# Gated cross-attention with a mixture of experts: pairwise scores in a new order, an output projection in two products per head, and a later first split

## What is computed

```python
q = (x @ Wq) ...; k = (context @ Wk) ...; v = (context @ Wv) ...        # 8 heads of 64
attn = softmax(einsum('bhnd,bhmd->bhnm', q, k) * scale)
out = einsum('bhnm,bhmd->bhnd', attn, v) ... @ Wo + bo
x = x + tanh(g_xattn[0]) * xattn(layernorm(x), ctx_1024, ...)
# router: softmax over 8 experts, top 2, capacity 1280 per expert by weight
pre, gate = h @ W1[e], h @ Wg[e];  y = (pre * silu(gate)) @ W2[e]
x = x + tanh(g_ffn[0]) * ffn(layernorm(x), ...)
```

## Time and profile before

| | |
|---|---|
| median of the runs | 1911.17 us |
| the profiled execution | 1914.74 us, span 1913.0 us, mean granted TensorE clock 0.973 |
| busy in the span: PE / weight loads / DVE / ACT / POOL | 91% / 85% / 73% / 59% / 36% |
| attention stage | about 35 to 1220 us |
| END, search and lists | about 1210 to 1264 us |
| experts | about 1264 us to the end |

### The profile page before, as it was taken

The page is one execution under the profiler, slowest core; times in us unless marked ns, Lnnn a source line. Parts: engine busy times, 40 slices in busy tenths (PEclk is TensorE's granted clock), DMA queues, the critical chain, the costliest instruction groups (busy, mean ns, idle before and its releaser), DMA issues. The chain is left out here.

```text
span 1913.0 us, 38524 instructions
## 1 busy us (share of the span) xinstructions
PE 1749.2 (91%) x12942; PEld 1629.6 (85%) x12943; DVE 1396.8 (73%) x2955; ACT 1124.2 (59%) x2259; POOL 686.6 (36%) x619
## 2 busy tenths in 40 slices
PE   5899998998998998998998999559999999999998
PEld 4788887987887887887887888459999999999998
DVE  5888888888898888889898888655545645555443
ACT  4767656666766666666776776334545545445443
POOL 3352344344244245244343433423332322333232
PEclk9999999999999999999999999779999999999999
DMA  6100001001011001000000002233133132231211
GB/s 180 34 12 12 23 24 35 23 23 35 12 34 35 12 23 40 18 23 31 16 23 28 18 23 76 91 104 98 30 100 94 28 99 62 61 98 28 33 28 28
DMA packets 65148, 85.88 MB, mean 45 GB/s; under 512 B 7208, under 2 KB 53800, under 8 KB 65008
## 3 DMA queue, kind: packets, MB, share of 16 engines
q1 hardware_dynamic: 47680, 64.08, 10.6%
q0 software_dynamic: 15984, 18.82, 5.6%
q10 hardware_dynamic: 1344, 1.20, 0.2%
HBM read 54.59 MB, written 29.48 MB: 44 GB/s over the span
## 5 line engine op out<-in xcount | busy, mean ns | idle before, releaser
L678 POOL TENSOR_SCALAR probs<-probs,row_rec 128x1024 f32<-128x1024 f32 x256 | 287.7, 1124 | 704.4 <-DVE row_rec L1501 673.9
L1036 ACT ACTIVATE pt_h<-turned 128x512 fp32r<-128x512 f32 x512 | 279.8, 597 | 199.1 <-PE turned L814 194.7
L1207 DVE TENSOR_TENSOR pt_l<-turned,pt_h 128x512 fp32r<-128x512 f32 x512 | 333.6, 684 | 78.4 <-ACT pt_h L1036 76.2
L1491 DVE TENSOR_REDUCE neg_max<-scores 128x1 f32<-128x1024 f32 x256 | 310.9, 1214 | 2.0 <-PE scores L801 1.9
L1120 ACT ACTIVATE probs<-scores,neg_max 128x1024 f32<-128x1024 f32 x256 | 287.2, 1122 | 3.4 <-DVE neg_max L1491 2.4
L814 PE MATMUL turned<-ident,probs 128*128 128x128 f32 x2048 | 272.6, 277 | 10.8 <-POOL probs L678 6.0
L915 PE MATMUL ring<-pt_h,v_hl 128*128 128x256 f32 x1024 | 254.0, 286 | 24.3 <-DVE q_l L1404 9.2
L1658 DVE TENSOR_TENSOR act_f<-ffn,silu 128x256 f32<-128x256 f32 x288 | 122.1, 424 | 193.1 <-ACT silu L1161 180.1
L814 PEld LDWEIGHTS turned<-ident,probs 128*128 128x128 f32 x2048 | 235.3, 143 | 23.5 <-POOL probs L678 10.2
L915 PE MATMUL ring<-pt_l,v_hl 128*128 128x256 f32 x1024 | 251.4, 284 | 0.0
L1161 ACT ACTIVATE silu<-ffn 128x256 f32<-128x256 f32 x288 | 110.4, 383 | 220.3 <-PE ffn L781 212.4
(11 more groups left out here) (219 smaller groups left out, 4514.6 us busy)
## 6 DMA issues: line engine op xcount, KB each, us to landing
w_raw<-w_t SPq DMA_DIRECT2D x16, 1024.0 KB, 8.4
e_rows<-lists SPq DMA_DIRECT2D x37, 260.0 KB, 2.7
ctx_raw<-ctx_t SPq DMA_DIRECT2D x16, 512.0 KB, 3.8
wg_raw<-wg_t SPq DMA_DIRECT2D x8, 1024.0 KB, 8.3
lists<-rows SPq DMA_DIRECT2D x8, 520.0 KB, 7.9
x_in<-x SPq DMA_DIRECT2D x8, 512.0 KB, 3.5
x_sum<-x SPq DMA_DIRECT2D x8, 512.0 KB, 3.5
out<-x_sum SPq DMA_DIRECT2D x8, 512.0 KB, 3.0
```

What stands on the lines that cost most here:

```text
L678: nc.gpsimd.tensor_scalar(probs[:, k, :], probs[:, k, :], row_rec[:, k:k + 1], 1.0, ALU.mult, ALU.mult).then_inc(scaled, 1)
L1036: return nc.scalar.activation(dst, src, ACT.Copy)
L1207: return nc.vector.tensor_tensor(dst, src, hi_part.bitcast(F32), ALU.subtract)
L1491: nc.vector.tensor_reduce(neg_max[:, k:k + 1], scores[:, k, :].rearrange("p (a c) -> p a c", a=2), AX.XY, ALU.max, negate=True).then_inc(n ...
```

## The change

Scores: units are now paired. Unit u is head 2 * (u // 8) + u % 2 and tokens u // 2 % 4, so that the even and the odd unit of a pair are two heads of the same tokens, which lie in the two halves of the partitions. `k_h`, `k_l`, `q_h`, `q_l` hold each part once, as the bank has it: one instruction of 128 partitions writes each on each engine. A pair's scores are 12 matmuls of 512 columns over 64 rows each, alternately on the lower and the upper half of the array's rows, issued together at the even unit once both exponentials of the last pair are done. The product of the two low parts is left out. POOL scales a pair at the even unit, DVE inverts a pair's sums in one instruction at the odd unit. `probs` has four places.

PE's order in a unit becomes scores (even units), transposes of u-2, jobs of u. `JOBS` is a new table, with at most two jobs beside an "o", and the "o" jobs stand at u % 4 in (1, 2). The context of the next batch is split on POOL at units 24 and 26 (20 and 23 before). The eight scatters of rows to the lists stand at units 29 and 30, four each (two each at 27 to 30 before).

Output projection: rows 0 to 63 of `ot_h` are the head's output times the high part of V, rows 64 to 127 times the low part. `ot_x` holds the high part of rows 0 to 63 below and the low part of the same rows above; `wo_x` holds the low part of the weights below and the high part above. Two passes of 256 columns per head replace three. ACT gets one more instruction of 64 partitions for each "o".

END: DVE waits for the last rows to be normalised before it splits the first expert's weights. END has 29 units instead of 27.

```diff
-            if u % 2 == 1 and (prev if u < 5 else own):
-                mine.append(("o", ((u - 5) % UNITS) // 2, 0))
+            if u % 4 in (1, 2) and (prev if u < 5 else own):
+                mine.append(("o", ((u - 5) // 4 * 2 + u % 4 - 1) % (2 * H), 0))
...
-                until(pe, exp_done, at(b, UNITS, u - 1))
-                for part in (q_h, q_l):
+                until(pe, exp_done, at(b, UNITS, u))
+                for n, (st, mv) in enumerate(((q_h, k_h), (q_h, k_l), (q_l, k_h))):
                     for half in range(2):
                         cols = slice(half * 512, (half + 1) * 512)
-                        last = nc.tensor.matmul(scores[:, u % 2, cols],
-                                                part[:, buf, ab, q * P:(q + 1) * P],
-                                                k_st[:, buf, ab, cols],
-                                                start=part is q_h, stop=part is q_l)
-                last.then_inc(scores_done, 1)
+                        for ab in range(2):
+                            head = slice(ab * DH, (ab + 1) * DH)
+                            last = nc.tensor.matmul(scores[:, ab, cols], st[head, buf, toks],
+                                                    mv[head, buf, cols], start=n == 0, stop=n == 2)
+                            if n == 2 and half == 1:
+                                last.then_inc(scores_done, 1)
...
-                        last = passes(bank[:, 0:D], (ot_h[:, h, toks], ot_l[:, h, toks]),
-                                      (wo_h[:, head, :], wo_l[:, head, :]), h == 0, h == H // 2 - 1)
+                        nc.tensor.matmul(bank[:, 0:D], ot_h[:, h, toks], wo_h[:, head, :],
+                                         start=h == 0, stop=False)
+                        last = nc.tensor.matmul(bank[:, 0:D], ot_x[:, h, toks], wo_x[:, head, :],
+                                                start=False, stop=h == H // 2 - 1)
...
-                    if body.own:
+                    if body.own and u % 2 == 0:
                         make_scores(body, u)
+                    if body.prev if u < 2 else body.own:
+                        turn(body, u - 2)
                     for what, c in jobs:
...
-                    if body.prev if u < 2 else body.own:
-                        turn(body, u - 2)
...
-                    for ab in range(2):
-                        for half in range(2):
-                            last = nc.scalar.activation(q_h[half * DH:(half + 1) * DH, i % 2, ab, :],
-                                                        bank[ab * DH:(ab + 1) * DH, :], ACT.Copy,
-                                                        scale=SCALE)
+                    last = nc.scalar.activation(q_h[:, i % 2, :], bank, ACT.Copy, scale=SCALE)
...
+                    if body.own and u % 2 == 1:
+                        exponent(b, u)
+                    for what, c in jobs[first:]:
+                        drain(body, u - 1, what, c)
+                    if body.prev if u < 2 else body.own:
+                        high_turned(b, u - 2)
+                    if body.own and u % 2 == 0:
+                        exponent(b, u)
...
+                    if body.own and u % 2 == 0:
+                        highest(b, u)
+                        highest(b, u + 1)
...
                     if body is END and u == 12:
 
+                        v.wait_ge(normed[1], at(b, QT, 0))
                         for i in range(3):
                             v.wait_ge(w_first_hi, i + 1)
```

More of the change, by code:

```diff
@@ L82 @@
 CONSTS = 16
-NEXT_FROM = 24
-END_STEPS = 27
+NEXT_FROM = 23
+SLOT_OF = {job: u for u, jobs in JOBS.items() for job in jobs}
+END_STEPS = 29
 class Body:
@@ L124, in place @@
     def place(self, job):
-        if job[0] != "x" and (job[1] > 0 or job == ("v", 0, 3)):
+        if SLOT_OF[job] < NEXT_FROM:
             return self.where[job]
@@ L502, in run @@
                 elif body.own:
-                    wait_filled(sp, body, body.where[("k", 3, 1)])
+                    wait_filled(sp, body, max(body.where[job] for job in
+                                              (("q", 3, 0), ("k", 3, 1), ("v", 1, 3))))
                     alone(sp)
@@ L692, in run @@
                             normalise(1, b - 1, x_sum, rows)
-                        if body.own and 27 <= u < 27 + QT:
-                            for k in range(2):
-                                scatter(b - 1, 2 * (u - 27) + k)
+                        if body.own and u in (29, 30):
+                            for k in range(QT):
+                                scatter(b - 1, QT * (u - 29) + k)
                         if u == UNITS - 1:
@@ L832, in wait_for_job @@
                         pe.wait_ge(weights_split, 5)
-                    reads = [body.where[("o", H * i + H - 2 + j // 2, 0)]]
+                    o = ("o", H * i + H // 2 + 1 + j // 2 * 2, 0)
+                    reads = [body.before.where[o] - RING if i == 1 and j < 2 else body.where[o]]
                 if kind == "x":
@@ L1096, in run @@
                             .then_inc(gate_exp, 1)
-                    for what, c in jobs[1:]:
-                        drain(body, u - 1, what, c)
                     if body is END and u == 8:
@@ L1487, in run @@
                     between(body, u, 1)
-                    if body.own:
-                        v.wait_ge(scores_done, at(b, UNITS, u + 1))
-                        nc.vector.tensor_reduce(neg_max[:, k:k + 1],
-                                                scores[:, k, :].rearrange("p (a c) -> p a c", a=2),
-                                                AX.XY, ALU.max, negate=True).then_inc(neg_done, 1)
-                    for what, c in jobs[1:]:
+                    if body.own and u % 2 == 1:
+                        k = (u - 1) % 4
+                        v.wait_ge(exp_done, at(b, UNITS, u + 1))
+                        nc.vector.reciprocal(row_rec[:, k:k + 2], row_sum[:, k:k + 2])\
+                            .then_inc(rec_done, 1)
@@ L1495, in run @@
+                    for what, c in jobs[first:]:
                         drain(body, u - 1, what, c)
                     between(body, u, 2)
-                    between(body, u, 3)
-                    if body.own if u > 0 else body.prev:
-                        v.wait_ge(exp_done, at(b, UNITS, u))
-                        nc.vector.reciprocal(row_rec[:, 1 - k:2 - k], row_sum[:, 1 - k:2 - k])\
-                            .then_inc(rec_done, 1)
+                    if body.prev if u < 2 else body.own:
+                        low_turned(b, u - 2, 0)
+                        between(body, u, 3)
+                        low_turned(b, u - 2, 1)
+                    else:
+                        between(body, u, 3)
```

193 lines of the change are left out of this document (109 added, 84 removed), and 7 rows, old and new, of the table JOBS.

## The result

The changed kernel took **1836.7 us** (median, 1834.9 to 1837.2) against 1914.0 for the kernel before in the same runs: a ratio of 0.9596, 95% interval 0.9573 to 0.9619, 4% faster. The forecast was 1783, with a range of 1731 to 1860. The direction and the range held; of the 128 us foreseen, 77 to 78 came. The measured time lies 2 us beyond the forecast's own end of 1835 and inside the range only by the room that two of the rivals had been given.

The account below looks back on a forecast made before the run. PE was taken as first bound, DVE second; a batch's period becomes 120.8 + 7.1 + 6.5 + 0.5 = 134.9 us. In all 1914.7 - 123 - 2 - 3 = 1786.7 us profiled, 1783 for the median, range 1731 to 1860.

Parts of the forecast that it names:

- the forecast's own end of 1835: Whole time if all 13.0 us of other waits and clock loss per batch stay: period 141.4 us.
- two of the rivals: Toll for changing row form, 1824 us, and queues becoming the bound, 1848 us; each about 1 in 8.
- The bound: Attention stage: PE first bound with 133.4 us issue time a batch, DVE second, 4 us behind in busy time.
- Scores: A pair's scores on PE: 1.47 us for 2.02 by overlap of the array's halves, saving 8.8 us a batch.
- the second rival: Toll at changes between 64-row and 128-row matmuls: 0.32 us a pair, 5.1 a batch, 1824 us total; about 1 in 8.
- Output projection: "w" jobs on PE: two passes per head for three, 3.8 us less of PE a batch.
- Waits: Per batch: 3.9 of 16.9 us lost go with the "q" drain, 6.5 of 13.0 kept, 7.1 and 0.5 added.
- 2.75 us less the even jobs: PE's wait at the odd unit's transposes for the even unit's lower halves: 7.1 us a batch.
- Period: Time per batch: 134.9 us, 15.4 less than 150.3; ends 128.4 and 141.4.
- Batch 0: First batch, counted among the eight that each get 15.4 us shorter, with no term of its own.
- START: First "v" no longer waits 3.25 us for a "q" drain of 2.79 us: -2 us (0 to -3).
- END: Waiting for POOL's normalisation before DVE's split ends that split at 1233.9 for 1237.1: -3 us (-3.5 to +2.3).

Follow-up runs that it names:

- The added product: Changed kernel with four more passes of 256 columns, overwritten by the next, at the head of every output projection job: 1851.0 us, ratio 0.9675.
- the run on one half: Changed kernel with both heads' score matmuls taken from the lower half of the partitions, same order: 2008.0 us in a single run.
- taking one maximum away from in front: On top of the late split, DVE's first lower half of the even unit put between a pair's two maxima: 1830.1 us, ratio 0.9563.
- Without the loop: On top of the late split, the six middle batches written out one after the other: 1812.8 us, ratio 0.9479.
- the late split: Changed kernel with DVE's two splits of the output weights in batch 0 moved from the head of units 5 and 9 to their end: 1823.0 us, ratio 0.9529.
- the two one-line runs: END's wait before the first expert's split added to the kernel before: 1909.4 us; taken from the changed kernel: 1839.4 us.
- full rows for the scores: Changed kernel with a pair's twelve 64-row score matmuls replaced by six of 128 rows: 1824.2 us in a single run.

## Why the prediction was right, and where it was off

- **The bound.** Right in kind: PE's issue time fell and the period with it. But PE was not as nearly the only bound as the sum took it. The added product shows half a microsecond of period for each of PE.
- **Scores.** The step "1.47 us a pair" measured 1.59, plus 0.10 ahead and 0.06 behind. The overlap is there, shown by the run on one half (2.97). The term was mis-sized by the toll, the second rival: it was priced at 0.32 us a pair and left out of the forecast; it is 0.35. PE's issue time becomes 120.8 + 16 x (1.59 - 1.47 + 0.10 + 0.06) = 125.3 us. That rival came true: 5.3 to 6.7 us in the last batch, and hidden by the jump's longer wait inside the loop.
- **Output projection.** PE's work fell as said; the time it is worth is 14 us, not 31.
- **Waits.** 138.0 - 125.3 = 12.7 us a batch are lost for 14.1 forecast, and this near hit is in part luck. `q_l` went as said. The rule "2.75 us less the even jobs" priced 7.1; 3.4 are seen. At unit 9 it is nearly right (1.2 us for 1.35). Its largest term, 1.95 us for slot 14, was a slip: that slot has an "o" job too (14 % 4 = 2), and no wait for `pt_l` stands behind it. There is none at units 1, 7, 21 and 31 either, and one of 1.2 us at unit 25, priced at 0.45. What makes the lower halves late is not settled: taking one maximum away from in front made it worse, and that this is so because all that follows a pair's second maximum came later is argued from ACT's longer wait. The loop's jump was in the trace before, among the 13 us that I halved without reading them: 5.1 us of waits for issue in five batches, and batch 6, behind which no jump stands, took 146.0 us where the five before it took 148.2 to 152.0. The wait of the earlier trace rows stood there too.
- **Period.** 138.0 for 134.9. Without the loop it is 135.2, so the jumps are 2.8 of these 3.1 us. The toll, 4.5 us of PE's issue time, was made up by smaller waits: 125.3 + 9.9 where 120.8 + 14.1 were forecast.
- **Batch 0.** The step that failed most plainly: it was taken as a batch like the others. Its two weight splits cost 13.7 us, and I had not followed what is queued behind a wait at the head of DVE's unit when ACT's part stands behind two exponentials. The same code stood in the kernel before, where DVE's waits were 1.75 and 2.67 us and are now 4.46 and 3.98. With the late split batch 0 takes 126.4 us; in proportion to the period it would be 136.4 x 138.0 / 150.3 = 125.2.
- **START.** The first scores start at 34.3 for 35.1 us: -0.8, not -2. The wait for the "q" drain went, but the first "v" starts at 24.6 for 25.05, behind a wait of 4.9 us for issue.
- **END.** -3 forecast; the rows show -4, the two one-line runs 2.1 and 2.7. Not foreseen: the last score matmul, at 1124.0, lies 21.4 us before the last store, where it was 1220.2 - 1201.8 = 18.4. With few jobs beside them a pair's lumps are bare: in the last units PE waited 3.6 us for `pt_l` and 2.6 for POOL's scaling, before at most 1.7 us there.
- **The sum.** The span fell by 78 us where 128 were forecast. By stretches, in us: START 0.8 for 2; batch 0 2.1 more where 15.4 less were forecast; batches 1 to 6 72.4 for 92.4 (897.5 to 825.1); batch 7 up to the last store 3.7 for 15.4 (151.2 to 147.5); behind it 3.6 for 3. So 20 of the 50 missing are in the period, 17.5 in batch 0 (12 of them the splits), 12 in the last batch, where PE's waits rose from 10 to 14 us and the rest is not taken apart, and 1 in START, less 1 in END.

## What to carry to other kernels

Matmuls over half the rows in two independent chains, into different banks, cost almost half if each has a partner on the other half; keep such stretches long, since the change of form costs about 0.35 us for going in and out. When units are made larger, look once more at what only the first and the last round do: a wait that was short beside small units can stand behind the larger lump on the other engine. Before a saving on the busiest engine is multiplied by the rounds, put a known piece of work back and see what it is worth. And when an edit is worth only 2 or 3 us in 1800, read it from the distance of the batches, since the stretches ahead of the loop differ by as much from one execution to the next.

## What was not expected of the hardware

- A matmul on the free half of the rows starts ahead of earlier ones that wait for the other half: with six of one head issued before six of the other, the seventh started 0.57 us after the first, and twelve took 2.16 us where 1.59 were taken in alternation and 2.97 with no partner.
- The jump back of a loop with a body of some 990 matmuls (and as many weight loads) held PE for up to 2.3 us each time, and cost 2 to 3 us from batch to batch (137 to 139 us for 135.2). With full rows for the scores the same jump held PE for about 5 us; why is open.
- POOL's multiply-add of 128x256 takes 0.55 us alone and 2 us while DVE subtracts 128x512 tiles in SBUF; DVE's four subtractions take 2.69 us then and 2.50 alone.
